# A fused two-layer graph network on one core: the passes through adj and layer 2 of groups 12 and 13 behind the last gates

## The chip, the cores and the metric

One Trainium2 chip, one of its cores. The time is the device time of one execution in microseconds (us), and it is given as the median of several runs. Engines are named as in the profile: PE is TensorE, DVE is VectorE, ACT is ScalarE, POOL is GpSimd, SP is SyncE, which only issues DMAs here.

## What is computed

64 graphs of 128 nodes with 128 features, all float32. `adj` is a symmetric 0/1 matrix for each graph.

```python
h = relu(layernorm(x))
# layer 1: a convolution over the nodes, messages between near nodes, and a gated unit
x_conv = relu(bn2(conv17(relu(bn1(conv1(h))))) + h)
s = h @ w_se.T + b_se;  A = exp(-squared_distances(s)) * adj
x_nmp = A @ relu(h @ w_msg.T + b_msg)
gi = [x_conv, x_nmp] @ w_ih.T + b_ih;  gh = h @ w_hh.T + b_hh
r, z = sigmoid(gi_r + gh_r), sigmoid(gi_z + gh_z)
x = x + (1 - z) * tanh(gi_n + r * gh_n) + z * h
# layer 2
h = relu(layernorm(x))
x = x + adj @ (h @ weight) + bias
```

## The kernel before

**Tiling.** The 64 graphs are 16 groups of four (NG = 16, GG = 4). A group is a tile of 128 x 512 (W = 512): the 128 partitions are nodes or features, and each 128 columns one graph. `x` and `adj` of a group come by one DMA of 256 KB each into rings of 8 and 6 slots; the result is built in the slot of `x` and stored from there. PSUM has eight banks of 128 x 512: pF, pH, pP, pQ, pZ, pI, and pN and pR, which are the two halves of the tensor pNR.

**Steps.** Each engine has a program of its own, in an order written out by hand, and the engines wait for each other by counting semaphores: `have(engine, s, n)` waits until s has reached n. After an opening come seven steps, t = 1 to 7. Step t does the convolution products and the gates of groups 2t and 2t + 1 ("middle"), the first part of groups 2t + 2 and 2t + 3 ("front"; there is none in step 7), and layer 2 of groups 2t - 2 and 2t - 1, called pp and qq. So step 7 does layer 2 of groups 12 and 13, and a function `ending` that of 14 and 15 (END = 15).

**Products** (`product`, L307; the matmuls are in `split_product`, L302 to 305). The convolution is nine products, each of 12 or 15 matmuls of 128 x 256 in three rounded parts. In step 7 PE's order is X22, X12, o_turn(13), X21, X23, adj_h2(12), X32, layer2(12), X11, adj_h2(13), X13, layer2(13), X31, X33, and then the gates of 14 and 15, each of 27 matmuls of 128 x 512. Two of these steps wait for more than their inputs. X11 waits for `between` on DVE (t_set), X31 for `scaled_third` on ACT (s32_set, L774), which reads bank pP before X31 overwrites it. ACT has second(13) ahead of it in its queue. Once the products are done, DVE adds the bases in two `conv_out` (L1101), of which the second needs POOL's last `sums` instruction (L1365).

**Layer 2 of a group** goes like this.
- `o_turn(g)` (PE, L468): four transposes of the gated result into pI or pH. It waits for `blend_end` (DVE, L1066 and L1068), which waits for `candidate` (ACT, L761), which waits for `blend_start` (DVE, L1056 to 1062).
- `residual(g)` (DVE, L1073) and `normalise2(g)` (DVE, L1079 to 1086) write x1 and its mean and variance, `scale2(g)` (POOL, L1302) the reciprocal root, `shift2(g)` (DVE, L1090) the bias `nb`, `second(g)` (ACT, L732, four instructions) the normalised h2[g % 2]. There are two buffers h2, so second(g) overwrites what layer2(g - 2) read.
- `adj_h2(g)` (PE, L475): the pass through adj, four matmuls into `back(g)`, which is pI for odd groups and pZ for even ones. `turned_up(g)` (ACT, L738) copies it back to h2[g % 2]. `layer2(g)` (PE, L483) multiplies by the weight, into the same bank.
- `with_bias(g)` (POOL, L1350) writes x1 plus the bias of layer 2 into the slot of `x`, `finish(g)` (DVE, L1096) adds the bank of layer2 to it, and SP stores the slot. SP's loop takes the groups in order.

In step 7 ACT's order is second(12), turned_up(12), second(13), scaled_third, turned_up(13), the gates. DVE's is ... shift2(12), normalise2(13), between, shift2(13), finish(12), finish(13), the gates.

**The ending.** The last group, 15, is done in two halves. On PE: 13 calls of `keep_clock` (L343, a matmul of 128 x 128 each, whose result nobody uses), o_turn(15), adj_h2(14), layer2(14), three calls of keep_clock, `end_pass` of both halves (L352, into pF and pQ), `end_layer2` of both halves (L361). On ACT: candidate(15), second(14), turned_up(14), the two halves of second(15) (L912), and the copies of their passes (L918, L920). On DVE: residual(14), normalise2(14), blend_start(15), shift2(14), blend_end(15), residual(15), normalise2_half(0) and (1) (L1241 to 1248), shift2_half(0) and (1) (L1252), finish(14), and the two last additions (L1270, L1272). On POOL: scale2(14), scale2_half(0), then, once DVE has written `nb` of half 0, scale2_half(1) (L1308), then, once `nb` of half 1 is there, with_bias(14) and with_bias(15).

In the profile a float32 matmul of 128 x 128 is recorded as two passes, so four of them are "x8"; a transpose is one.

Of the kernel before, what the change touches and what calls it, by code (L numbers as in the profile page):

```python
# [38 lines left out]
def gnn_kernel(nc, x_in, adj_in, vec_in, early_in, conv_in, gate_in, late_in, bias_in, out):  # L39
    ctx = ExitStack()  # L40
    with ctx:
# [147 lines left out]
        def graph(t, j):  # L189
            return t[:, j * N:(j + 1) * N]  # L190
# [3 lines left out]

        END = NG - 1

        end_pass_bank, end_out_bank = (pF, pQ), (pH, pP)

        def back(g):
            return (pI if g % 2 else pZ)[:]  # L200

        def two(t, e):
            return t[:, 2 * e * N:2 * (e + 1) * N]
# [97 lines left out]
        def _(pe):  # L301
# [43 lines left out]
            def end_pass(e):  # L345
                if e == 0:
                    pe.wait_ge(h2_half, 1)
                    have(pe, tz_set, END + 1)
                else:
                    have(pe, h2_set, END + 1)  # L350
                for j in (2 * e, 2 * e + 1):
                    last = pe.matmul(graph(end_pass_bank[e], j), graph(h2[END % 2], j), adjs(END, j), start=True, stop=True)  # L352
                last.then_inc(uT_done if e else uT_half_done, 1)

            def end_layer2(e):
# [62 lines left out]
            def gates_h(g):  # L418
                if g == 0:
                    pe.wait_ge(gate_split, 1)  # L420
                if g % 2 == 0:
                    have(pe, msg_set, min(g + 4, NG))
                    have(pe, out_set, g - 1)
                else:
                    have(pe, ghn_set, g)
                gate_part(pN, 2, 2, half(h_hi, g), half(h_lo, g), True, True).then_inc(hidden_done, 1)
                if g % 2:
                    have(pe, tr_set, g)
                gate_part(pR, 2, 0, half(h_hi, g), half(h_lo, g), True, False)
                if g == 0:  # L430
                    have(pe, nlo_set, 2)
                gate_part(z_bank(g)[:], 2, 1, half(h_hi, g), half(h_lo, g), True, False)
# [10 lines left out]
            def gates_n_i(g):  # L443
                if g % 2:
                    have(pe, v_set, g)
                else:
                    have(pe, out_set, g)
                gate_part(pI[:], 1, 2, half(n_hi, g), half(n_lo, g), True, False)

            def gates_c(g):  # L450
# [2 lines left out]
                gate_part(pR, 0, 0, m_hi, m_lo, False, True).then_inc(r_done, 1)  # L453
                gate_part(pI[:], 0, 2, m_hi, m_lo, False, True).then_inc(i_done, 1)
                gate_part(z_bank(g)[:], 0, 1, m_hi, m_lo, False, True).then_inc(z_done, 1)

            def back_bank(g):
                return pI if g % 2 else pZ

            def o_turn(g):  # L460
                have(pe, oT_set, g + 1)
# [9 lines left out]
            def adj_h2(g):  # L471
                have(pe, h2_set, g + 1)
                have(pe, tz_set, g + 1)
                for j in range(GG):
                    last = pe.matmul(graph(back_bank(g), j), graph(h2[g % 2], j), adjs(g, j), start=True, stop=True)  # L475
                last.then_inc(uT_done, 1)

            def layer2(g):
                if g == 0:
                    pe.wait_ge(late_loaded, 16)  # L480
                have(pe, uT_set, g + 1)
                for j in range(GG):
                    last = pe.matmul(graph(back_bank(g), j), graph(h2[g % 2], j), w_l1, start=True, stop=True)  # L483
                last.then_inc(l1_done, 1)

            def opening():
# [66 lines left out]
            def step(t):  # L553
                a, b, p, q, pp, qq = 2 * t + 2, 2 * t + 3, 2 * t, 2 * t + 1, 2 * t - 2, 2 * t - 1
                front, middle = t + 1 < NS, t < NS
                if t == 1:
                    pe.wait_ge(w_split, 6)
                if middle:
                    have(pe, cxlo_set, cx_before(t) + 1)
                    have(pe, ct_set, 2 * t)  # L560
                    product(pP, 0, X22, four(M22, True))
                if front:
                    x_turn(b)
                    conv1(a)
                    messages(a)
                if middle:
                    have(pe, cxlo_set, cx_before(t) + 2)
                    product(pP, 1, X12, four(M12, True)).then_inc(f_done[0], 1)
                o_turn(qq)
                if front:  # L570
                    conv1(b)
                    messages(b)
                    rows_turn(a)
                if middle:
                    have(pe, tz_set, 2 * t)
                    product(pQ, 0, X21, four(M21, True))
                if front:
                    distances(a)
                if middle:
                    have(pe, cxlo_set, cx_before(t) + 3)  # L580
                    product(pQ, 1, X23, four(M23)).then_inc(f_done[1], 1)
                adj_h2(pp)
                if front:
                    rows_turn(b)
                if middle:
                    have(pe, s1_set, t)
                    product(pP, 0, X32, four(M32)).then_inc(f_done[2], 1)
                layer2(pp)
                if middle:
                    have(pe, cxlo_set, cx_before(t) + 5)  # L590
                    have(pe, t_set, t)
                    product(pQ, 0, X11, four(A0, True))
                if front:
                    distances(b)
                    neighbour_sums(a)
                adj_h2(qq)
                if middle:
                    product(pQ, 1, X13, four(A2)).then_inc(f_done[3], 1)
                layer2(qq)
                if front:  # L600
                    neighbour_sums(b)
                if middle:
                    have(pe, s32_set, t)
                    product(pP, 0, X31, four(A1))
                    product(pP, 1, X33, four(A3)).then_inc(f_done[4], 1)
                    gates_h(p)
                    gates_n(p)
                    gates_c(p)
                    gates_h(q)
                    if t + 2 < NS:  # L610
                        x_turn(a + 2)
                    gates_n_rz(q)
                    if not front:
                        o_turn(p)
                    gates_n_i(q)
                    if front:
                        o_turn(p)
                    gates_c(q)

            def ending():  # L620
                have(pe, ct_set, 2 * NS)
                have(pe, xclo_set, 2 * NS)
                keep_clock(13)
                o_turn(END)
                adj_h2(END - 1)
                layer2(END - 1)
                keep_clock(3)
                end_pass(0)
                end_pass(1)
                end_layer2(0)  # L630
                end_layer2(1)
# [7 lines left out]
        def _(act):  # L639
# [227 lines left out]
            def step(t):  # L867
# [14 lines left out]
                if front:  # L882
                    decay(a)
                    messages(b)
                    left_rows(b)
                turned_up(pp)
                second(qq)
                if front:
                    split_hi(t + 1, 0)
# [3 lines left out]
                if front:  # L893
                    decay(b)
                    sums_hi(a)
                turned_up(qq)
                if t + 2 < NS:
                    first(a + 2)
                    first(b + 2)
# [3 lines left out]
                    gates(t)  # L903

            def ending():
                candidate(END)
                second(END - 1)
                turned_up(END - 1)
                for j in range(GG):
                    if j % 2 == 0:  # L910
                        act.wait_ge(nb2_set, END + 1 + j // 2)
                    last = act.activation(graph(h2[END % 2], j), graph(x1[END % 2], j), ACT.Relu,  # L912
                                          bias=nb2[END % 2][:, j:j + 1], scale=rs2[END % 2][:, j:j + 1])
                    if j == 1:
                        last.then_inc(h2_half, 1)
                last.then_inc(h2_set, 1)
                act.wait_ge(uT_half_done, 1)
                act.activation(two(h2[END % 2], 0), two(end_pass_bank[0], 0), ACT.Copy).then_inc(uT_half_set, 1)  # L918
                have(act, uT_done, END + 1)
                act.activation(two(h2[END % 2], 1), two(end_pass_bank[1], 1), ACT.Copy).then_inc(uT_set, 1)  # L920
# [28 lines left out]
        def _(dve):  # L949
# [119 lines left out]

            def residual(g):  # L1070
                have(dve, o_placed, g + 1)
                have(dve, out_set, g - 1)
                dve.scalar_tensor_tensor(x1[g % 2], (pI if g % 2 else pH)[:], 0.5, xs(g), ALU.mult, ALU.add)\  # L1073
                   .then_inc(x1_set, 1)

# [122 lines left out]
            def step(t):  # L1198
# [22 lines left out]
                shift2(qq)  # L1221
                if front:
                    right_rows(b)
                finish(pp)
                if front:
                    split_lo(t + 1, 0)
                    split_lo(t + 1, 1)
                    masked(b)
                    sums_lo(a)
                finish(qq)  # L1230
                if front:
                    sums_lo(b)
                if middle:
# [21 lines left out]
            def ending():  # L1255
# [6 lines left out]
                residual(END)  # L1262
                normalise2_half(0)
                normalise2_half(1)
                shift2_half(0)
                shift2_half(1)
                finish(p)
                have(dve, x1b_set, END + 1)
# [180 lines left out]
```

## Time and profile before

| | us |
|---|---|
| median of 3 runs | 347.70 |
| lowest and highest of them | 345.97 and 348.69 |
| the profiled execution | 345.98 |
| its span, first to last instruction | 344.1 |
| last gate's last matmul starts | 330.20 |
| last addition on DVE ends | 341.74 |

The times of the rows are counted from the start of the profiled execution's span. A row of a timeline gives the start, the length, the engine, the line of the kernel, the operation, the tiles written and read, how many such instructions are taken together, and in brackets how long the engine was idle before it and what ended the idle time. Buffer numbers are left out, so `work` stands for tr, tz, cand, zh, x1 and h2, and x_ring for any slot. The ends of matmuls are modelled and overlap the next start; starts are the better measure of PE's pace. The granted clock is the share of TensorE's full clock.

### The profile page before, as it was taken

The page shows a single profiled execution, that of the slowest core. Times are in us where ns is not written, and L with a number is a line of the kernel's source. Part 1 is how long each engine was busy: PE and PEld are TensorE (multiplying, and loading weights), DVE is VectorE, ACT ScalarE, POOL GpSimd, SP SyncE. Part 2 cuts the span into 40 slices and gives each one's busy share as a digit, 9 for nine tenths or more (in the row PEclk, how much of TensorE's full clock was granted, in tenths as well). Part 3 has the DMA queues.
Part 4 walks back from the last instruction along what each step waited for, and adds up shares of the span by engine and source line. Part 5 has one row for each costly group of instructions (what it writes and reads, how often), then busy time and mean ns, then how long its engine had stood idle before and what let it go on. Part 6 is the DMA issues. An engine that isn't in the chain of part 4 may idle for free.

```text
span 344.1 us, 6334 instructions
## 1 busy us (share of the span) xinstructions
PE 331.1 (96%) x2212; PEld 297.5 (86%) x2212; DVE 263.2 (76%) x735; ACT 220.8 (64%) x431; POOL 151.7 (44%) x131
## 2 busy tenths in 40 slices
PE   8699979999999999999999999999999999999995
PEld 5489968799989998899989998899989998899884
DVE  5597987898688976898688977898677968674473
ACT  2958745977775785667775785667776655452443
POOL 7053370035932297035922297036920396055014
PEclk9999999999999999999999999999999999999999
DMA  7900100001310031001210031001100000001001
GB/s 233 339 4 0 61 33 0 2 1 53 102 33 1 3 122 63 0 0 59 99 31 0 4 123 61 0 2 61 65 0 2 0 32 30 3 0 63 0 1 64
DMA packets 7952, 15.04 MB, mean 44 GB/s; under 512 B 1008, under 2 KB 1648, under 8 KB 7792
## 3 DMA queue, kind: packets, MB, share of 16 engines
q1 hardware_dynamic: 7776, 14.62, 12.4%
q8 instruction: 18, 0.29, 0.4%
q14 instruction: 14, 0.11, 0.1%
q10 hardware_dynamic: 144, 0.01, 0.0%
HBM read 10.43 MB, written 4.19 MB: 43 GB/s over the span
## 4 chain that ended last, share of the span: by engine, by line
issue 41%; POOL 30%; PE 13%; DVE 9%; ACT 5%; DMA 1%; POOLq 1%; DVEq 0%; ACTq 0%
POOL x_ring L1350 5%; POOL base L1362 3%; POOL rs L1297 3%; POOL ac L940 3%; POOL px L944 2%; POOL px L934 2%; POOL px L937 2%; POOL base L1365 2%; POOL rs L1302 2%; POOL base L1356 2%; DMA vec<-vec_in 1%; PE pNR L305 1%; PE pNR L303 1%; PE pNR L304 1%; ACT conv_hi L658 1%
## 5 line engine op out<-in xcount | busy, mean ns | idle before, releaser
L1302 POOL TENSOR_TENSOR rs<-ve,neg_half 128x4 f32<-128x4 f32 x15 | 15.6, 1039 | 94.7 <-DVE ve L1086 94.7
L1297 POOL TENSOR_TENSOR rs<-ve,neg_half 128x8 f32<-128x8 f32 (+1 forms) x9 | 15.5, 1720 | 73.0 <-DVE ve L964 73.0
L303 PE MATMUL pP<-cx_hi,conv_hi 128*128 128x256 f32 x154 | 45.1, 293 | 0.0
L305 PE MATMUL pP<-cx_hi,conv_lo 128*128 128x256 f32 x154 | 43.5, 282 | 0.0
L304 PE MATMUL pP<-cx_lo,conv_hi 128*128 128x256 f32 x154 | 43.3, 281 | 0.0
L303 PE MATMUL pQ<-cx_hi,conv_hi 128*128 128x256 f32 x126 | 37.2, 295 | 0.0
L305 PE MATMUL pQ<-cx_hi,conv_lo 128*128 128x256 f32 x126 | 35.4, 281 | 0.0
L304 PE MATMUL pQ<-cx_lo,conv_hi 128*128 128x256 f32 x126 | 35.4, 281 | 0.0
L732 ACT ACTIVATE work<-work,nb,rs 128x128 f32<-128x128 f32 x60 | 24.8, 483 | 15.1 <-DVE nb L1090 15.1
L303 PEld LDWEIGHTS pP<-cx_hi,conv_hi 128*128 128x128 f32 x154 | 29.1, 189 | 0.3
L304 PEld LDWEIGHTS pP<-cx_lo,conv_hi 128*128 128x128 f32 x154 | 29.1, 189 | 0.3
L305 PEld LDWEIGHTS pP<-cx_hi,conv_lo 128*128 128x128 f32 x154 | 29.0, 188 | 0.0
L1045 DVE TENSOR_TENSOR cx_lo<-px,cx_hi 128x576 fp32r<-128x576 f32 x28 | 27.2, 1009 | 0.8 <-ACT cx_hi L646 0.8
L304 PEld LDWEIGHTS pQ<-cx_lo,conv_hi 128*128 128x128 f32 x126 | 23.8, 189 | 0.3
L303 PEld LDWEIGHTS pQ<-cx_hi,conv_hi 128*128 128x128 f32 x126 | 23.8, 189 | 0.0
L305 PEld LDWEIGHTS pQ<-cx_hi,conv_lo 128*128 128x128 f32 x126 | 23.7, 188 | 0.0
L752 ACT ACTIVATE work<-pNR,rz_b 128x512 f32<-128x512 f32 x16 | 11.0, 689 | 19.5 <-PE pNR L305 19.0
L665 ACT ACTIVATE hn<-x_ring,nb,rs 128x128 f32<-128x128 f32 x56 | 22.5, 485 | 0.0
L1350 POOL TENSOR_TENSOR x_ring<-work,late 128x512 f32<-128x512 f32 x16 | 20.4, 1278 | 0.3 <-DVE nb L1252 0.3
L1096 DVE TENSOR_TENSOR x_ring<-pI,x_ring 128x512 f32<-128x512 f32 x7 | 4.8, 692 | 20.2 <-POOL x_ring L1350 15.9
L646 ACT ACTIVATE cx_hi<-px 128x576 fp32r<-128x576 f32 x28 | 17.6, 674 | 3.6 <-POOL px L942 3.1
L761 ACT ACTIVATE work<-work,vec 128x512 f32<-128x512 f32 x16 | 11.6, 724 | 11.4 <-DVE work L1059 11.4
(275 smaller groups left out, 1071.7 us busy)
## 6 DMA issues: line engine op xcount, KB each, us to landing
x_ring<-x_in SPq DMA_DIRECT2D x16, 256.0 KB, 2.8
adj_ring<-adj_in SPq DMA_DIRECT2D x16, 256.0 KB, 3.0
out<-x_ring SPq DMA_DIRECT2D x15, 256.0 KB, 2.0
work<-conv_in SPq DMA_DIRECT2D x1, 1088.0 KB, 8.0
x_ring<-gate_in SPq DMA_DIRECT2D x1, 576.0 KB, 7.6
out<-x_ring SPq DMA_DIRECT2D x2, 128.0 KB, 1.8
early<-early_in SPq DMA_DIRECT2D x1, 129.5 KB, 3.4
late<-late_in SPq DMA_DIRECT2D x1, 128.0 KB, 7.9
```

What stands on the lines that cost most here:

```text
L303: pe.matmul(acc, w_hi, m_hi, start=start, stop=False)
L304: pe.matmul(acc, w_hi, m_lo, start=False, stop=False)
L305: return pe.matmul(acc, w_lo, m_hi, start=False, stop=stop)
L646: act.activation(cx_hi[:, CX_PARTS[k][0]:CX_PARTS[k][1]], cx_source(k), ACT.Copy).then_inc(cxhi_set, 1)
L665: last = act.activation(graph(hn[g % 2], j), xs(g, j), ACT.Identity, bias=nb1[:, i:i + 1], scale=rs1[:, i:i + 1])
L732: last = act.activation(graph(h2[g % 2], j), graph(x1[g % 2], j), ACT.Relu, bias=nb2[g % 2][:, j:j + 1], scale=rs2[g % 2][:, j:j + 1])
L752: act.activation(tr, pR, ACT.Tanh, bias=rz_b[:, 0:1], scale=0.5).then_inc(tr_set, 1)
L761: act.activation(cand[g % 2], cand[g % 2], ACT.Tanh, bias=vec[:, V_IN:V_IN + 1], scale=1.0)\
L1045: dve.tensor_tensor(cx_lo[:, part], cx_source(k), cx_hi[:, part].bitcast(F32), ALU.subtract)\
L1297: pool.tensor_tensor(rs1[:, lane], ve1[:, lane], neg_half[:, lane], ALU.pow).then_inc(rs1_set, 1)
L1302: pool.tensor_tensor(rs2[g % 2][:], ve2[g % 2][:], neg_half[:, 0:GG], ALU.pow).then_inc(rs2_set, 1)
L1350: pool.tensor_tensor(xs(g).rearrange("p (g d) -> p g d", g=GG), x1[g % 2].rearrange("p (g d) -> p g d", g=GG), l1_bias, ALU.add).then_inc( ...
```

## The change

Layer 2 of groups 12 and 13 (LATE) is begun but not finished in step 7. Both passes through adj go behind the last gates on PE, both layer2 behind them, in place of most of the filler; ACT's copies and DVE's finishes go to the ending too. The passes get banks of their own, pN for group 12 and pF for group 13, so the last pass of group 15 takes pR instead of pF. Waits for out_set in the gates and in residual are changed accordingly.

The first `ending` below is PE's, the second ACT's, the third DVE's; in `step` the same condition stands before turned_up on ACT and finish on DVE, for pp and for qq.

```diff
-        end_pass_bank, end_out_bank = (pF, pQ), (pH, pP)
+        end_pass_bank, end_out_bank = (pR, pQ), (pH, pP)
+        LATE = (END - 3, END - 2)
+        def back_bank(g):
+            if g in LATE:
+                return (pN, pF)[g % 2]
+            return pI if g % 2 else pZ
         def back(g):
-            return (pI if g % 2 else pZ)[:]
+            return back_bank(g)[:]
...
             def gates_h(g):
-                    have(pe, out_set, g - 1)
+                    have(pe, out_set, g - 1 if g < END - 1 else g - 3)
             def gates_n_i(g):
-                    have(pe, out_set, g)
+                    have(pe, out_set, g if g < END - 1 else g - 2)
             def adj_h2(g):
                 have(pe, h2_set, g + 1)
                 have(pe, tz_set, g + 1)
+                if g in LATE:
+                    have(pe, nlo_set, NG)
+                    have(pe, ghn_set, NG)
...
             def step(t):
-                adj_h2(pp)
+                if pp not in LATE:
+                    adj_h2(pp)
-                layer2(pp)
+                if pp not in LATE:
+                    layer2(pp)
...
             def ending():
+                adj_h2(END - 3)
+                adj_h2(END - 2)
                 have(pe, ct_set, 2 * NS)
                 have(pe, xclo_set, 2 * NS)
-                keep_clock(13)
+                keep_clock(2)
+                layer2(END - 3)
+                keep_clock(4)
                 o_turn(END)
+                layer2(END - 2)
                 adj_h2(END - 1)
                 layer2(END - 1)
                 keep_clock(3)
...
             def ending():
+                turned_up(END - 3)
                 candidate(END)
+                turned_up(END - 2)
+                have(act, l1_done, END - 2)
                 second(END - 1)
                 turned_up(END - 1)
+                have(act, l1_done, END - 1)
...
             def residual(g):
-                have(dve, out_set, g - 1)
+                have(dve, h2_set, g - 1)
+                have(dve, x1b_set, g - 1)
...
             def ending():
                 normalise2_half(0)
                 normalise2_half(1)
+                finish(END - 3)
                 shift2_half(0)
+                finish(END - 2)
                 shift2_half(1)
                 finish(p)
```

## Rows read from the trace of the kernel before

**Rows 1.** The page, its first part: busy time and share of each engine.
```profile
PE 331.1 (96%) x2212; PEld 297.5 (86%) x2212; DVE 263.2 (76%) x735; ACT 220.8 (64%) x431; POOL 151.7 (44%) x131
```

**Rows 2.** Windows of the ending: length, then each engine's busy time, granted clock, DMA.
```profile
330.40:333.70 3.30, 3.10 (x27) 2.87 (x25) 3.06 (x6) 2.91 (x6) 1.20 (x1) 1.00 0.00 0
333.70:341.30 7.60, 6.05 (x42) 5.10 (x42) 3.66 (x15) 3.10 (x8) 3.88 (x4) 1.00 0.01 3
```

**Rows 3.** Timeline of PE, last step: start, length, what, idle time before it.
```profile
305.58 0.28 PE L304 MATMUL pQ<-cx_lo,conv_hi 128*128 128x256 f32 x1
305.70 0.28 PE L305 MATMUL pQ<-cx_hi,conv_lo 128*128 128x256 f32 x1
306.20 1.16 PE L475 MATMUL pZ<-adj_ring,work 128*128 128x128 f32 x8 [0.22 <-ACT work L732]
307.12 0.36 PE L303 MATMUL pP<-cx_hi,conv_hi 128*128 128x256 f32 x1
...
308.63 1.05 PE L483 MATMUL pZ<-late,work 128*128 128x128 f32 x8
309.44 0.36 PE L303 MATMUL pQ<-cx_hi,conv_hi 128*128 128x256 f32 x1
309.64 0.28 PE L304 MATMUL pQ<-cx_lo,conv_hi 128*128 128x256 f32 x1
```

**Rows 4.** Timeline of PE, ending.
```profile
330.43 3.06 PE L343 MATMUL pP<-ident 128*128 128x128 f32 x26
333.70 0.75 PE L468 MATMUL pI<-ident,work 128*128 128x128 f32 x4 [0.21 <-DVE work L1068]
334.29 1.06 PE L475 MATMUL pZ<-adj_ring,work 128*128 128x128 f32 x8
336.03 1.16 PE L483 MATMUL pZ<-late,work 128*128 128x128 f32 x8 [0.69 <-ACT work L738]
337.03 0.83 PE L343 MATMUL pP<-ident 128*128 128x128 f32 x6
338.12 0.71 PE L352 MATMUL pF<-adj_ring,work 128*128 128x128 f32 x4 [0.26 <-ACT work L912]
```

**Rows 5.** Timeline of ACT, last step and ending.
```profile
309.82 0.55 ACT L774 ACTIVATE s<-pP,bn_half,bn_a 128x256 f32<-128x256 f32 x1
...
331.48 0.72 ACT L761 ACTIVATE work<-work,vec 128x512 f32<-128x512 f32 x1 [0.16 <-DVE work L1059]
332.15 1.65 ACT L732 ACTIVATE work<-work,nb,rs 128x128 f32<-128x128 f32 x4
335.38 0.60 ACT L738 ACTIVATE work<-pZ 128x512 f32<-128x512 f32 x1 [1.58 <-PE pZ L475]
337.19 0.88 ACT L912 ACTIVATE work<-work,nb,rs 128x128 f32<-128x128 f32 x2 [1.21 <-DVE nb L1252]
```

**Rows 6.** Timeline of POOL, last step and ending.
```profile
312.12 1.29 POOL L1365 TENSOR_TENSOR base<-base,s 128x512 f32<-128x512 f32 x1
...
337.49 0.70 POOL L1308 TENSOR_TENSOR rs<-ve,neg_half 128x2 f32<-128x2 f32 x1 [0.53 <-DVE nb L1252]
338.46 2.49 POOL L1350 TENSOR_TENSOR x_ring<-work,late 128x512 f32<-128x512 f32 x2 [0.27 <-DVE nb L1252]
```

**Rows 7.** Timeline of DVE, last step and ending.
```profile
314.74 0.69 DVE L1096 TENSOR_TENSOR x_ring<-pI,x_ring 128x512 f32<-128x512 f32 x1 [4.32 <-PE pI L483]
315.35 0.75 DVE L1101 SCALAR_TENSOR_TENSOR pQ<-pQ,bn_a,base 128x512 f32<-128x512 f32 x1
...
317.57 0.76 DVE L1101 SCALAR_TENSOR_TENSOR pP<-pP,bn_a,base 128x512 f32<-128x512 f32 x1
...
332.96 0.69 DVE L1068 TENSOR_TENSOR work<-work 128x512 f32<-128x512 f32 x1
...
336.99 0.16 DVE L1252 SCALAR_TENSOR_TENSOR nb<-mv,rs 128x2 f32<-128x2 f32 x1
```

**Rows 8.** The page, its last part: DMA issues, size, time to landing.
```profile
out<-x_ring SPq DMA_DIRECT2D x15, 256.0 KB, 2.0
```

More of the change, by code:

```diff
@@ L348, in end_pass @@
                     have(pe, tz_set, END + 1)
+                    have(pe, tr_set, END + 1)
                 else:
@@ L351, in end_pass @@
                 for j in (2 * e, 2 * e + 1):
-                    last = pe.matmul(graph(end_pass_bank[e], j), graph(h2[END % 2], j), adjs(END, j), start=True, stop=True)
+                    last = pe.matmul(graph(end_pass_bank[e][:], j), graph(h2[END % 2], j), adjs(END, j), start=True, stop=True)
                 last.then_inc(uT_done if e else uT_half_done, 1)
@@ L455, in gates_c @@
                 gate_part(z_bank(g)[:], 0, 1, m_hi, m_lo, False, True).then_inc(z_done, 1)
-            def back_bank(g):
-                return pI if g % 2 else pZ
             def o_turn(g):
@@ L473, in adj_h2 @@
                 have(pe, tz_set, g + 1)
+                if g in LATE:
+                    have(pe, nlo_set, NG)
+                    have(pe, ghn_set, NG)
                 for j in range(GG):
-                    last = pe.matmul(graph(back_bank(g), j), graph(h2[g % 2], j), adjs(g, j), start=True, stop=True)
+                    last = pe.matmul(graph(back(g), j), graph(h2[g % 2], j), adjs(g, j), start=True, stop=True)
                 last.then_inc(uT_done, 1)
@@ L482, in layer2 @@
                 for j in range(GG):
-                    last = pe.matmul(graph(back_bank(g), j), graph(h2[g % 2], j), w_l1, start=True, stop=True)
+                    last = pe.matmul(graph(back(g), j), graph(h2[g % 2], j), w_l1, start=True, stop=True)
                 last.then_inc(l1_done, 1)
@@ L595, in step @@
                     neighbour_sums(a)
-                adj_h2(qq)
+                if qq not in LATE:
+                    adj_h2(qq)
                 if middle:
                     product(pQ, 1, X13, four(A2)).then_inc(f_done[3], 1)
-                layer2(qq)
+                if qq not in LATE:
+                    layer2(qq)
                 if front:
@@ L885, in step @@
                     left_rows(b)
-                turned_up(pp)
+                if pp not in LATE:
+                    turned_up(pp)
                 second(qq)
@@ L895, in step @@
                     sums_hi(a)
-                turned_up(qq)
+                if qq not in LATE:
+                    turned_up(qq)
                 if t + 2 < NS:
@@ L1223, in step @@
                     right_rows(b)
-                finish(pp)
+                if pp not in LATE:
+                    finish(pp)
                 if front:
@@ L1229, in step @@
                     sums_lo(a)
-                finish(qq)
+                if qq not in LATE:
+                    finish(qq)
                 if front:
```

## The prediction

> **What bounds the kernel now.** I read the page first. PE is busy for 331.1 of 344.1 us, 96%, and no other engine is above 76% [rows 1], so matmul time that leaves PE's queue should come off the span wherever no other engine is just behind it. The timeline of PE in the last step (t = 7) bears this out: pieces of products follow each other every 0.12 us, and the only idle time around the first moved pass is 0.22 us before 306.20 [rows 3]. The ending is another regime. In its first 3.3 us PE counts as busy for 3.10, but 26 of its 27 passes there are filler; in the following 7.6 us it is busy for 6.05 and waits for DVE once and for ACT again and again [rows 2, 4]. So the ending is a chain that runs through several engines, and PE's work there is free only up to its filler and its waits. In the two timelines of POOL and DVE the reader should see the chain's last links: the second reciprocal root at 337.49, which waited for DVE's `nb` of 336.99, and then the two bias additions, 2.49 us from 338.46 [rows 6, 7].
>
> All times below are on the clock of before; the shift that the last step gives is taken off at the end.
>
> **Part 1: 16 matmuls leave the last step.** adj_h2(12), layer2(12), adj_h2(13) and layer2(13) are four matmuls each, recorded as eight passes. What one costs is read from the starts around it. L305 at 305.70 would be followed by the next product 0.12 later, at 305.82. Instead there is the pass from 306.20 and X32 begins at 307.12, and the first matmul behind such a block takes 0.20 instead of 0.12 (309.44 to 309.64), so 0.08 more: 307.12 + 0.08 - 305.82 = 1.38 us, the wait for h2 included. The second goes from 308.63 to 309.44, plus 0.08: 0.89 us [rows 3]. The third and the fourth look the same. Sum: 1.38 + 3 x 0.89 = **4.05 us**.
>
> Can the last step use it? Three things could be late next.
> - Product X31 begins 1.38 + 0.89 + 0.89 = 3.16 us earlier, at 310.45, and must have s32, which ACT writes from 309.82 for 0.55, so until 310.37 [rows 5]. With the 0.05 us from engine to engine (DVE ends at 332.96 + 0.69, PE starts at 333.70 [rows 4, 7]) that is 310.42: 0.03 us to spare. ACT does not come to it sooner, because it first has the normalisation of group 13.
> - DVE's second conv_out stands at 317.57 behind the last product; 4.05 earlier is 313.52. POOL's sum for it starts at 312.12 and takes 1.29, until 313.41 [rows 6, 7]. 0.1 us to spare.
> - The finishes of 12 and 13 leave DVE ahead of conv_out (314.74, the next at 315.35, so 0.61 us each [rows 7]); DVE waited 4.32 us there, so this brings nothing more.
> So I take the full 4.05, with almost no reserve. The gates behind it move together with what they wait for. Their waits on out_set are lowered by as much as the finishes are moved, and cost nothing. The two waits that residual has in place of its one on out_set are fulfilled whenever DVE comes to them; I take 0, and at most 0.1 for the additional wait in the ending.
>
> **Part 2: the same passes in PE's ending.** The filler's pass rate: 26 passes last 3.06, 6 last 0.83, so one takes (3.06 - 0.83) / 20 = 0.111 us [rows 4]. Before, 13 fillers are 26 passes from 330.43, 2.9 us, issued by 333.3; then o_turn(15) waits for DVE until 333.70. Now there are 8 + 8 (both passes through adj), 4 (two fillers), 8 (layer2(12)) and 8 (four fillers) ahead of o_turn: 36 passes, 4.0 us, issued by 334.43. Is anything else later than that? The first pass through adj is done at 330.43 + 7 x 0.111 + 0.27 (the tail of a pass, 0.83 - 5 x 0.111) = 331.48. ACT then copies uT(12), 331.52 to 332.12 at the 0.60 of its row at 335.38, and only behind it candidate(15), which stood at 331.48 [rows 5]. An ACT instruction starts a little before the one ahead of it ends (331.48 + 0.72 = 332.20, the next at 332.15), so I put it at 332.04: 0.56 us late. DVE's end of the blend, 332.96 for 0.69 [rows 7], is late by the same and releases o_turn at 333.70 + 0.56 = 334.26. That is before 334.43, so PE's own queue decides: o_turn starts **0.73 us later**. Bounds: 0.56 (DVE alone) and 1.05 (if four changes of kind cost 0.08 each, as behind the blocks of rows 3). I take 0.73 because all of these passes are of the filler's kind. layer2(12) does not stall PE: uT(12) is there at 332.12, and PE comes to it at 332.65.
>
> **Part 3: ACT and PE between o_turn and the halves of group 15.** second(14) now waits for layer2(12), done at 333.54 + 0.16 = 333.70; it starts at 333.74, 1.59 later than at 332.15, and ends at 335.39 [rows 5]. PE meanwhile does o_turn (0.59, 333.70 to 334.29 [rows 4]) and layer2(13), 0.89, until 335.91, and the pass of group 14 until 336.80. ACT copies it, 337.01 to 337.61; layer2(14) takes PE 1.00 (336.03 to 337.03 [rows 4]) from 337.64, and three fillers 0.67, until 339.31. The first half pass of group 15, which must not be late, stood at 338.12; by the sum of parts 2 and 4 it is due at 339.46. That leaves 0.15 us of the cover. I take 0; if turned-up copies and passes each cost a little more, 0.1 to 0.4 us.
>
> **Part 4: finish(12) stands ahead of `nb` on DVE.** At 336.99 DVE came straight from the variance and wrote `nb` of the first half [rows 7]. Now finish(12), 0.61 us to the next start (314.74 to 315.35), goes first: **0.61 us**. Behind `nb` wait ACT's first half (337.19), and POOL's second root (337.49), then POOL's bias additions and the last finishes, so nothing hides it. finish(13) lies in the time in which POOL computes the second root, 0.70 us, and is hidden: DVE has it done at about 339.1 and the root at 339.5. Bounds of this term: 0.69, and 0.35, since POOL started 0.34 after `nb` ended [rows 6, 7], where other engines need 0.05; if some 0.26 of that is POOL's own preparation, it absorbs that much. The POOL part is one chain of two, so I take 0.61.
>
> **Part 5: stores.** The outputs of 12 and 13 now leave at about 338.4 and 339.1, with some 2.0 us each to landing [rows 8], and those of 14 and 15 from 341.9. They are gone, or nearly, when the last half is issued at 343.1. I take 0, at most 0.3.
>
> **The sum.** The profiled execution took 345.98 us, with 1.9 us around its span of 344.1. 345.98 - 4.05 + 0.73 + 0.61 = **343.3 us**, a ratio of 0.992. The median of the three runs shown is 347.7, 0.5% above the profiled one; 347.7 x 0.992 = **345.0 us**.
>
> **The rivals.**
> *The last step does not give its 4.05 us.* s32 (0.03 to spare) or POOL's sums hold the products up. For it: these margins. Against: a late sum of POOL is caught before gates_c, which does not need it until more than 1 us later. A loss goes one for one; with 0.7 us lost, 344.0 profiled and 345.7 us.
> *The ending hides everything.* If o_turn and `nb` had room that the timelines don't show, all 4.05 us would arrive: 341.9 profiled, 343.6 us. For it: a third of the ending is waits and filler [rows 2]. Against: parts 2 and 4 each found a queue with nothing between.
> *Slower: PE's clock falls in the ending.* Real passes stand where an unbroken row of 26 filler passes stood, and now PE waits for ACT between them. The granted clock is 1.00, the 2.4 GHz level, in both windows of the ending, although PE is idle there for 1.5 of 7.6 us [rows 2]. Were it at the 1.2 GHz level from the gates on, the 36 passes would take 4.0 us more. Then o_turn, layer2(13), the pass, layer2(14) and three fillers, 34 passes or 3.8 us more, and 8 passes of the halves, 0.9 us: 345.98 - 2.7 + 8.7 = 352.0 profiled, 353.7 us. It decides from 2.7 / 0.111 = 24 slow passes on. Against: the new waits, 0.8 us at most, are hardly longer than the 0.69 of before [rows 4].
> The Trainium skill (TensorE: Matmul & The Clock Gate, section "What's actually happening") speaks for this rival: "the default state is throttled, and activity releases the throttle". The waits of 0.2 to 0.7 us in rows 4 did not bring the clock down, so this trace does not show the fall.
>
> **How the numbers follow.** The forecast gets 0.73, the last step's loss 0.12, the full gain 0.10, the clock 0.05. The bounds of the terms give gains from 1.6 us (1.05 and 0.69 lost, 0.4 in part 3, 0.3 elsewhere) to 3.1 us (0.56 and 0.35 lost). On the median that is 344.6 to 346.1, and the three runs of before lie 1.7 below and 1.0 above their median; together with the full gain, the range is 342.5 to 347.6 us. One per cent, 3.5 us, is about what a measurement of this kernel can tell from no change. The forecast's 2.7 us is under it, and by scatter passes it one time in four (0.19); with most of the full gain (0.08) and a little of the second case that is 0.28 for faster. Slower by over 1% is the clock alone, 0.04. Within 1%: 0.68.
>
> **What would show it.** In the last step PE's starts around X32, X11, X13 and X31 without the blocks, the first filler-like pass at 326.4, and no new wait ahead of X31. In the ending, o_turn(15) 4.0 us behind the end of the gates rather than 3.3 (3.8 would say that DVE decides). ACT's candidate(15) straight behind the copy of pN. DVE: finish(12) between the variance and `nb`, 0.61 us. A wait of PE ahead of the first half pass of under 0.2 us. Wrong would be: an idle PE in front of X31, a granted clock below 1.00 behind the gates, or a first half pass that follows the fillers without a wait, which would mean that part 3 has become the bound.

## The result, and the profile after

The median of 16 runs is 345.52 us, against 347.72 us for 16 runs of the kernel before beside them: 2.20 us less. The runs of a kernel lie in steps some 1.5 us apart, and the two middle runs of the changed kernel, 345.04 and 346.01, lie on either side of such a step, so this difference is a poor measure. The ratio of the two kernels is 0.9918, with an interval from 0.9899 to 0.9936, and that is 2.85 us; it leaves out one run of the changed kernel, which at 348.26 us was a slow one. The forecast was 345.0 us and a ratio of 0.992.

The profiled execution took 344.95 us with a span of 342.6, so only 1.5 us less than that of before. To compare the two, one has to know first where the clock of each was low. ACT's `scaled_first` of the last step, ahead of everything that the change touches, in the timeline of ACT of the kernel before and then of the changed one:

```profile
302.32 0.56 ACT L767 ACTIVATE s<-pP,bn_half,bn_a 128x256 f32<-128x256 f32 x1 [2.01 <-PE pP L305]
```

```profile
303.84 0.56 ACT L785 ACTIVATE s<-pP,bn_half,bn_a 128x256 f32<-128x256 f32 x1 [2.00 <-PE pP L313]
```

The changed kernel comes there 1.52 us later. The windows of its opening say why (length, busy time and count of PE, PEld, DVE, ACT, POOL, granted clock, DMA share, GB/s):

```profile
14.00:18.00 4.00, 1.87 (x12) 1.53 (x11) 3.83 (x6) 3.94 (x7) 0.00 (x0) 1.00 0.61 228
18.00:22.00 4.00, 4.00 (x13) 3.09 (x12) 3.75 (x28) 0.76 (x2) 1.38 (x1) 0.57 0.02 4
22.00:26.00 4.00, 4.00 (x24) 3.47 (x23) 2.21 (x6) 1.99 (x4) 3.92 (x4) 1.00 0.01 2
```

From 18 to 22 us the granted clock was 0.57 on average: mostly its 1.2 GHz level, behind a stretch in which PE was busy for 1.87 of 4 us. In the profile of before it is 1.00 in the same windows, with the same wait of 2.13 us ahead of them. Other runs of before show such steps too, so I don't put this down to the edit of the last step; the experiments come back to it. The 1.52 us are taken out of the comparison, and 344.1 + 1.52 - 342.6 = 3.02 us is what the change gained between the two profiles.

The ending of the changed kernel in PE's timeline (start, length, what; it answers to [rows 4]):

```profile
327.98 1.05 PE L484 MATMUL pNR<-adj_ring,work 128*128 128x128 f32 x8
328.86 1.06 PE L484 MATMUL pF<-adj_ring,work 128*128 128x128 f32 x8
329.76 0.61 PE L351 MATMUL pP<-ident 128*128 128x128 f32 x4
330.20 1.06 PE L492 MATMUL pNR<-late,work 128*128 128x128 f32 x8
331.10 1.06 PE L351 MATMUL pP<-ident 128*128 128x128 f32 x8
331.99 0.64 PE L474 MATMUL pI<-ident,work 128*128 128x128 f32 x4
...
335.11 1.16 PE L492 MATMUL pZ<-late,work 128*128 128x128 f32 x8 [0.69 <-ACT work L756]
336.10 0.83 PE L351 MATMUL pP<-ident 128*128 128x128 f32 x6
336.93 0.52 PEld L361 LDWEIGHTS pNR<-adj_ring,work 128*128 128x128 f32 x4 [0.19 <-ACT work L936]
336.93 0.71 PE L361 MATMUL pNR<-adj_ring,work 128*128 128x128 f32 x4
```

From `scaled_first` to the end of the gates it is 28.11 us before (302.32 to 330.43) and 24.14 us now (303.84 to 327.98), so the last step gave 28.11 - 24.14 = 3.97 us. o_turn(15) stands 4.01 us behind the gates, without a wait, instead of 3.27: **0.74 us lost** to PE's own queue. The first half pass of group 15 shows no wait in PE's row, where it had 0.26 us, but that is the modelled end of the fillers: at 0.111 us for each of the six passes from 336.10 PE would have come to it at 336.77, and it started at 336.93, together with its weight load, which waited for ACT. So 0.16 us of the cover are left.

ACT's timeline ([rows 5]):

```profile
329.06 0.60 ACT L756 ACTIVATE work<-pNR 128x512 f32<-128x512 f32 x1 [0.20 <-PE pNR L484]
329.56 0.71 ACT L779 ACTIVATE work<-work,vec 128x512 f32<-128x512 f32 x1
...
331.30 1.65 ACT L750 ACTIVATE work<-work,nb,rs 128x128 f32<-128x128 f32 x4 [0.54 <-PE pNR L492]
```

The candidate stands straight behind the copy, 1.58 us behind the gates instead of 1.05, and second(14) waits for layer2(12), 3.32 behind the gates instead of 1.72.

DVE's timeline, and then POOL's, between the variance and the last addition ([rows 6, 7]):

```profile
335.15 0.69 DVE L1121 TENSOR_TENSOR x_ring<-pNR,x_ring 128x512 f32<-128x512 f32 x1
335.76 0.15 DVE L1279 SCALAR_TENSOR_TENSOR nb<-mv,rs 128x2 f32<-128x2 f32 x1
335.82 0.68 DVE L1121 TENSOR_TENSOR x_ring<-pF,x_ring 128x512 f32<-128x512 f32 x1
336.72 0.16 DVE L1279 SCALAR_TENSOR_TENSOR nb<-mv,rs 128x2 f32<-128x2 f32 x1 [0.21 <-POOL rs L1337]
...
339.83 0.41 DVE L1301 TENSOR_TENSOR x_ring<-pP,x_ring 128x256 f32<-128x256 f32 x1
```

```profile
335.99 0.70 POOL L1337 TENSOR_TENSOR rs<-ve,neg_half 128x2 f32<-128x2 f32 x1 [0.84 <-DVE nb L1279]
```

finish(12) lies ahead of `nb` as forecast. From o_turn to `nb` it is 3.77 us instead of 3.29, **0.48 lost**: 0.61 by the two starts above, less 0.11 by which o_turn is shorter when PE comes to it without a wait (0.64 against 0.75), and less 0.02 that I can't place. POOL's root follows `nb` after 0.23 instead of 0.50, start to start: **0.27 absorbed**. From the root to the last addition it is 3.84 us in both, and from that addition's end to the end of the span 2.36 in both, so the stores cost nothing. The account: -3.97 + 0.74 + 0.48 - 0.27 = -3.02.

### The profile page after: what moved, and what is told of

It reads as the page before. It is cut to its first block, busy times and chain, and to the rows that moved or that the text cites. A ratio compares the mean times of both kernels' runs of the same rounds, so it can differ in the third digit from the quotient of the medians.

```text
span 342.6 us, 6310 instructions
## 1 busy us (share of the span) xinstructions
PE 329.8 (96%) x2198; PEld 296.3 (86%) x2198; DVE 261.6 (76%) x735; ACT 220.5 (64%) x431; POOL 152.1 (44%) x131
## 4 chain that ended last, share of the span: by engine, by line
PE 65%; DVE 19%; ACT 9%; issue 4%; POOL 1%; DMA 1%; POOLq 0%; DVEq 0%; ACTq 0%
PE pQ L311 4%; PE pQ L312 4%; PE pQ L313 4%; PE pNR L311 4%; PE pNR L313 4%; PE pNR L312 4%; PE pF L424 4%; PE pP L311 4%; PE pP L312 4%; PE pP L313 4%; DVE st L981 3%; ACT work L750 2%; PE pZ L484 2%; PE pI L313 2%; PE pI L311 2%
## 5 line engine op out<-in xcount | busy, mean ns | idle before, releaser
L399 PEld LDWEIGHTS pNR<-early,hn 128*128 128x128 f32 x128 | 16.3, 189 | 3.0 <-issue 2.1
```

Source lines behind the costliest of these rows:

```text
L399: last = pe.matmul(ms[:, j, 0:MS], graph(hn[g % 2], j), w_ms, start=False, stop=True, skip_group_check=True)
```

## The experiments

Positions in a trace are counted from the ending's first pass through adj (327.98 in the profile above), so that the clock of the opening does not enter. In the changed kernel o_turn(15) is at 4.01 and the last addition at 11.85.

### The ending: e1, e2, e4

e1_finish_behind:

```diff
-                finish(END - 3)
                 shift2_half(0)
-                finish(END - 2)
                 shift2_half(1)
+                finish(END - 3)
+                finish(END - 2)
```

> The changed kernel with finish(12) and finish(13) behind both shift2 halves on DVE. My theory: finish(12) ahead of the first `nb` holds it up by 0.59 us, of which POOL's own preparation absorbs 0.27, so the last addition comes 0.3 us earlier, counted from the first pass through adj of the ending; the two finishes fit in the 1.45 us in which DVE waits for POOL's bias additions. Rival 1: POOL follows `nb` whenever it comes, then the whole 0.6 us is gained. Rival 2: the stores of 12 and 13 now run together with those of 14 and 15 and give it back behind the last addition, 0.3 us or more. Time: 0.1% less than the changed kernel, which cannot be told in the time, only in the trace.

DVE and then POOL in its timelines; its first pass is at 328.14:

```profile
335.34 0.16 DVE L1279 SCALAR_TENSOR_TENSOR nb<-mv,rs 128x2 f32<-128x2 f32 x1
...
339.68 0.42 DVE L1301 TENSOR_TENSOR x_ring<-pP,x_ring 128x256 f32<-128x256 f32 x1
```

```profile
335.82 0.70 POOL L1337 TENSOR_TENSOR rs<-ve,neg_half 128x2 f32<-128x2 f32 x1 [0.52 <-DVE nb L1279]
```

`nb` comes 7.20 behind the first pass instead of 7.78, 0.58 earlier, but the root then starts 0.32 behind its end instead of 0.08. The last addition is at 11.54: 0.31 us earlier, not 0.6. So rival 1, the whole 0.6 us, falls. From the last addition's start to the span's end it is 2.82 us (342.5 - 339.68) instead of 2.77: rival 2 has 0.05 us. (Ratio to before 0.9884, interval 0.9855 to 0.9913.)

e2_no_filler:

```diff
                 layer2(END - 3)
-                keep_clock(4)
                 o_turn(END)
```

> The changed kernel without the four fillers ahead of o_turn(15). My theory: PE's queue decides o_turn, by little; without the 8 passes (0.9 us) DVE decides, and o_turn comes 0.2 us earlier (DVE was done at 331.72, o_turn stood at 331.99), not 0.9. Rival 1: the filler was the whole delay, then 0.7 to 0.9 us are gained. Rival 2: PE's clock falls behind a gap of 0.7 us, then the granted clock in the ending is below 1.00 and the time 1 to 5 us longer.

PE's timeline, with the first pass at 326.53, and the windows behind the gates:

```profile
330.33 0.75 PE L474 MATMUL pI<-ident,work 128*128 128x128 f32 x4 [0.52 <-DVE work L1091]
```

```profile
326.40:330.30 3.90, 3.41 (x30) 3.18 (x28) 3.16 (x6) 2.83 (x6) 1.29 (x1) 1.00 0.00 2
330.30:338.20 7.90, 6.94 (x50) 5.99 (x50) 4.79 (x17) 4.21 (x11) 3.89 (x4) 1.00 0.18 67
```

o_turn waits for DVE again and comes at 3.80, 0.21 us earlier. By the last addition (338.28, so 11.75) 0.10 of it is left, because the o_turn behind a wait takes 0.75 again. The clock stays at 1.00 up to PE's last matmul. Both rivals fall; the ratio, 0.9926 (0.9902 to 0.995), cannot tell 0.1 us.

e4_full_filler has `keep_clock(11)` in that place.

> The changed kernel with 11 fillers instead of 4 ahead of o_turn(15), so 13 calls in all, as before the change. My theory: o_turn stands in PE's own queue, so 14 passes cost 1.55 us one for one: ratio to the kernel before 0.9962 instead of 0.9918, and the wait of PE ahead of the first half pass is no longer. Rival (the ending hides what PE does there): under 0.5 us.

PE's timeline; the first pass is at 328.32:

```profile
333.90 0.64 PE L474 MATMUL pI<-ident,work 128*128 128x128 f32 x4
```

o_turn at 5.58, 1.57 us later, and the last addition (341.75) at 13.43, 1.58 later. One for one: the ending hides none of it. The ratio was 0.9933 (0.9908 to 0.9959), and the expected 0.9962 lies just outside: by the times alone the cost would be less than by the trace. Of its six runs two had a clock of 1.00, spans 342.8 and 343.0, against 341.1 for the one such run of the changed kernel, and that agrees with the trace.

### The last step alone: e3, e8

e3_last_step_alone, an edit of the kernel before:

```diff
-                for j in range(GG):
+                for j in range(GG if g not in (END - 3, END - 2) else 1):
                     last = pe.matmul(graph(back_bank(g), j), graph(h2[g % 2], j), adjs(g, j), start=True, stop=True)
```

and the same in layer2.

> The kernel before, with one matmul in place of four in each of adj_h2(12), layer2(12), adj_h2(13) and layer2(13), everything else in its place: 12 of the 16 matmuls are left out (three of four graphs of groups 12 and 13 are not computed), and the ending is untouched. My theory: the last step gives one for one: 24 passes of 0.111 us, 2.7 us, ratio 0.992. Rival: the last step is held by ACT's s32 or POOL's sums, then there is an idle PE ahead of X31 and the gain is 2 us or less.

From adj_h2(12) to the first filler it is 24.23 us in the kernel before (306.20 to 330.43). Here, in PE's timeline:

```profile
308.12 0.49 PE L475 MATMUL pZ<-adj_ring,work 128*128 128x128 f32 x2 [0.22 <-ACT work L732]
...
321.49 0.50 PE L303 MATMUL pNR<-xc_hi,gate_hi 128*128 128x512 f32 x1 [0.42 <-DVE xc_lo L1105]
...
330.45 3.06 PE L343 MATMUL pP<-ident 128*128 128x128 f32 x26
```

22.33 us, a gain of 1.90, not 2.66; ratio 0.9952 (0.9931 to 0.9973). PE waits in front of gates_c(14) for DVE, but not for the reasons that the prediction feared. DVE's timeline:

```profile
316.69 0.69 DVE L1096 TENSOR_TENSOR x_ring<-pI,x_ring 128x512 f32<-128x512 f32 x1 [5.72 <-POOL x_ring L1350]
317.30 0.75 DVE L1101 SCALAR_TENSOR_TENSOR pQ<-pQ,bn_a,base 128x512 f32<-128x512 f32 x1
```

finish(13) stands in DVE's queue ahead of conv_out and waits for POOL's with_bias(13), which is behind all of POOL's sums. So the products were ready and their additions were not made. The trace of before already had this, in POOL's timeline:

```profile
313.36 1.27 POOL L1350 TENSOR_TENSOR x_ring<-work,late 128x512 f32<-128x512 f32 x1
```

It ends at 314.63, and PE's layer2(13), which the row of finish(13) names as what it waited for, at 313.61 + 1.05 = 314.66. POOL was only 0.03 us ahead of PE, so with PE's part taken away the wait would hardly have been shorter. e8_finish13_later leaves e3 as it is and moves that one instruction:

```diff
             def step(t):
-                finish(qq)
+                if middle and not front:
+                    pass
+                else:
+                    finish(qq)
...
             def gates(t):
                 conv_lo_out(t, 1)
+                if t == NS - 1:
+                    finish(2 * t - 1)
```

> The kernel of e3_last_step_alone (12 of the 16 matmuls in the last step left out, three of four graphs of groups 12 and 13 not computed) with finish(13) on DVE behind both conv_out and conv_lo_out of step 7 instead of ahead of them. e3 gained about 1.9 us where 2.7 were expected; its trace shows PE idle for 0.42 us in front of gates_c(14), and DVE's finish(13) waiting for POOL's with_bias(13) until 316.6. My theory: finish(13), not the products, held the conv_out behind it, so that the change of the study gained its 4 us only because it took the finishes out of the way too; here the wait in front of gates_c goes and the executions at full clock have a span of 341.5 (2.7 less than 344.2), or 343.1 with one stretch of low clock. Rival: POOL's sums or ACT's s32 hold the step, then the span stays at about 342.2 and 343.9.

PE's timeline:

```profile
309.49 0.49 PE L475 MATMUL pZ<-adj_ring,work 128*128 128x128 f32 x2 [0.23 <-ACT work L732]
...
322.31 0.40 PE L303 MATMUL pNR<-xc_hi,gate_hi 128*128 128x512 f32 x1
...
331.17 3.06 PE L343 MATMUL pP<-ident 128*128 128x128 f32 x26
```

The wait is gone and the stretch is 21.68 us: 2.55 less than before, against the 2.66 of 24 passes. The ratio was 0.9892 (0.9853 to 0.9931). None of its four runs had a clock of 1.00 throughout, so the span of 341.5 wasn't seen; the nearest, at 0.998, has 341.9, and the two at 0.994 have 343.0 and 343.3 for the 343.1 that was expected. So the last step does give one for one, or nearly, but only where finish(13) is no longer ahead of conv_out in DVE's queue. (finish(12) stayed where it was.)

How near the next limit was shows in the changed kernel itself, ACT's s32 and PE around the start of X31:

```profile
311.34 0.55 ACT L792 ACTIVATE s<-pP,bn_half,bn_a 128x256 f32<-128x256 f32 x1
```

```profile
311.86 0.28 PE L313 MATMUL pQ<-cx_hi,conv_lo 128*128 128x256 f32 x1
311.98 0.35 PE L311 MATMUL pP<-cx_hi,conv_hi 128*128 128x256 f32 x1
312.16 0.28 PE L312 MATMUL pP<-cx_lo,conv_hi 128*128 128x256 f32 x1
```

s32 is written at 311.89, and X31 starts 0.12 us behind the matmul ahead of it, as without a wait; its own first matmul takes 0.06 us longer than the others. No run moves s32 by itself.

### The clock of the opening: e5, e6, e7, e9, f1, f2

The runs of each kernel lie about 1.5 us apart, and the mean granted clock goes with it. Of the 16 runs of the changed kernel one has 1.00 and a span of 341.1, seven 0.995 and 342.5 to 342.9, seven 0.99 and 344.1 to 344.4, one 0.988 and 346.5. Where the clock falls, by the windows of e1's profile (0.99, the two stretches):

```profile
10.00:14.00 4.00, 3.25 (x11) 2.48 (x12) 0.69 (x1) 4.00 (x8) 0.00 (x0) 0.73 1.03 402
14.00:18.00 4.00, 3.49 (x21) 3.17 (x21) 3.77 (x5) 3.94 (x8) 0.00 (x0) 0.84 0.55 205
48.00:52.00 4.00, 3.02 (x14) 2.97 (x15) 2.44 (x16) 2.61 (x5) 3.04 (x3) 0.67 0.00 0
52.00:56.00 4.00, 4.00 (x19) 3.28 (x18) 2.21 (x5) 1.11 (x2) 0.00 (x0) 0.90 0.00 0
```

PE has two waits of some 2 us there: for the first products, until 17, and for distances(3), until 49. The second stretch, from 49.3, lies right behind the second wait. So does, in the profile of the changed kernel, the stretch from 18.3 behind the first wait (2.13 us, until 16.87). But the first stretch of e1 lies ahead of that wait, from 11.9 to 15.3, behind waits of 0.2 to 0.75 us; PE's row of the first products:

```profile
17.02 0.47 PE L337 MATMUL pQ<-cx_hi,conv_hi 128*128 128x512 f32 x1 [0.51 <-DVE cx_lo L1063]
```

They start when they do in the kernel before, at 17.04 there, so that stretch cost nothing: the slow fillers used up the wait. e5_opening_after and e6_opening_before fill the first wait:

```diff
                 messages(0)
-                keep_clock(6)
+                keep_clock(15)
                 pe.wait_ge(w_split, 1)
```

> The changed kernel with 15 fillers instead of 6 in the opening, ahead of the first products: 18 more passes, 2.0 us, in the 2.1 us in which PE waits there. In the profiled run of the changed kernel the granted clock was 0.58 and 0.57 from 18 to 22 us and 1.00 around it, the step of 1.52 us by which the last step begins later than in the profiled run of before. My theory: the wait and the thin work around it let the clock fall for a stretch in most runs, and with the filler it does not: runs at 341 us of span, the fastest of before the edit, and a median some 1.5 to 3 us less. Rival 1: the clock falls by something that the filler does not touch, then the runs keep their spans at 341, 342.6 and 344.2. Rival 2: the filler delays the first products and costs 0.2 to 1 us.

> The same edit of the opening alone, in the kernel before. My theory: its runs lie 1.5 us apart for the same reason (345.97, 347.6 and 349.1), so the median falls by the same amount, to about 346, ratio 0.995 or less; the changed kernel with the same edit stays 2.7 to 3.0 us below it. Rival: no difference, the scatter of before has another cause.

e5: 343.17 us, ratio 0.9866 (0.9824 to 0.9909), three of four runs at 1.00 with spans of 341.2 to 341.4. e6: 345.98 us, ratio 0.9951 (0.9923 to 0.9979), seven of eight at 1.00 with 344.1 to 344.3. The filler costs nothing: 344.1 is the span of before at 1.00. So both medians fell because fewer runs had a stretch of low clock. Between the two, 345.98 - 343.17, it is 2.81 us, where 2.7 to 3.0 were expected. In e6 the second wait was still there, 2.04 us in its profile, and yet only one of eight runs had a stretch, so the wait alone does not bring the clock down.

e7_all_three has the edits of e5, e1 and e2 together.

> The changed kernel with the filler of the opening, without the four fillers ahead of o_turn(15), and with the finishes behind the halves. My theory: 0.2 + 0.3 us from the ending and 1.5 to 3 us from the opening, so 2 to 3.5 us less than the changed kernel, ratio to before 0.983 to 0.986. Rival: the gap in the ending lets the clock fall there and takes back 1 us or more.

343.39 us, ratio 0.9859 (0.9827 to 0.9891). Its last addition (338.00, first pass at 326.57) is at 11.43, 0.42 us earlier than in the changed kernel, and three runs at 1.00 have 340.8. The rival, a clock that falls in the ending, did not come. The other three are at 0.995 and 342.3 or 342.4, so a stretch of low clock still came in half of them. e9_second_gap adds

```diff
-                distances(3)
-                neighbour_sums(2)
                 direct(15)
+                distances(3)
+                neighbour_sums(2)
```

> The kernel of e7_all_three with direct(15) ahead of distances(3) and neighbour_sums(2) in the opening. In the profiles with a second stretch of low clock it lies at 48 to 54 us, behind PE's wait of 2.0 to 2.2 us for distances(3) at 49. direct(15), nine matmuls and 1.5 us, is ready and can lie in that wait. My theory: the wait shrinks to some 0.6 us, the work behind it comes 1.4 us earlier and the low clock at 48 to 54 us does not come again: nearly all executions at a clock of 1.00 and a span of 339.4, median 341.2. Rival 1: POOL or ACT hold the first step anyway and the 1.4 us are lost again, span 340.8. Rival 2: the low clock comes elsewhere, then spans 1.5 us apart remain.

PE's timeline in place of the wait of 2.03 us:

```profile
47.80 0.40 PE L339 MATMUL pP<-cx_hi,conv_lo 128*128 128x512 f32 x1
48.85 0.50 PE L415 MATMUL pH<-right,left 128*128 128x512 f32 x1 [0.65 <-ACT left L736]
```

All six runs have 0.999 or 1.00, spans of 339.5 to 339.8, and the median is **341.50 us**, ratio 0.9804 (0.9778 to 0.9829): the fastest version here. With the clock steady, the change of this study can be measured to a tenth: f1_steady_before and f2_steady_after are the two kernels with both edits of the opening and nothing else.

> The kernel before with both edits of the opening (15 fillers ahead of the first products, direct(15) ahead of distances(3)) and nothing else. My theory: these edits take away the stretches of low clock, whatever stands in the ending: all executions within 0.3 us of each other, span 342.8 (344.2 less 1.4), time 344.7. Rival: the executions keep lying 1.5 us apart, as in the kernel before.

> The changed kernel with the same two edits. My theory: span 339.8, time 341.7, so that the change of the study is worth 3.0 us (0.87%) when the clock is out of the comparison, and the two small edits of the ending (e1, e2) are worth 0.4 us less than nothing of noise: e9 is 0.3 to 0.4 us below this one. Rival: 2.7 us, as forecast without POOL's absorption; or the change had been faster only by the chance of its runs' clocks, then under 2 us.

f1: 344.78 us, eleven of twelve runs between 344.64 and 345.04 (one at 0.993 and 346.21). f2: 341.83 us, six runs between 341.68 and 342.01. The change is worth 344.78 - 341.83 = **2.95 us**, 0.86%, and e1 and e2 together the 0.33 us by which e9 is below f2, although these two were not run side by side. Both profiles of the pair are at full clock, 0.999 and 1.00, so the account of the result can be made again with nothing taken out: from `scaled_first` to the end of the gates 28.09 and 24.13 us, from there to o_turn 3.27 and 4.01, to `nb` 3.29 and 3.77, to POOL's root 0.51 and 0.23, to the last addition 3.84 in both. That is -3.96 + 0.74 + 0.48 - 0.28 = -3.02 us once more.

Of the 18 runs of e5, e6 and e7, with the filler alone, 13 were at 1.00; of the kernel before, in the four sets of runs beside the experiments, 10 of 60. Of the 24 runs of e9, f1 and f2, with both edits of the opening, all but one were at 0.998 or more. The filler's effect is beyond chance. That direct(15) adds to it is likely, but 5 runs of 18 against 1 of 24 don't prove it, and no run has direct(15) alone. It also takes 1.2 us off the span at full clock (e7 to e9, 340.8 to 339.6), where 1.4 were expected.

## Why the prediction was right

**Part 1, the last step:** 4.05 forecast, 3.97 measured. X31 did have its 0.03 us to spare, nearly (0.06 lost). One sentence of this part was wrong: that the departure of the finishes from DVE's queue "brings nothing more". e3 and e8 show that for finish(13) it is a condition of the gain. Between adj_h2(12) and the filler it was worth 0.65 us already with 12 of the 16 matmuls away. I had read DVE's wait of 4.32 us at finish(13) as time to spare. But conv_out stands behind that instruction, and with the products 4 us earlier finish(13) would have waited until 314.63 for POOL. That the full gain came is in this respect luck: the change had to move finish(13) only because its input comes later.

**Part 2, PE's filler:** 0.73 forecast, 0.74 measured; e4 shows one for one, and e2 that DVE stands 0.21 us behind, for a forecast difference of 0.17.

**Part 3:** second(14) is the 1.6 us late that were forecast, and it costs nothing. The candidate is 0.53 late, for 0.56. The cover of the first half pass was put at 0.15 us, and by the starts it is 0.16. PE's row without a wait looks like the sign of being wrong that the prediction named, but it isn't: ACT released that pass. In e1, where `nb` is earlier, PE and not ACT's half decides that pass (8.79 behind the first pass, no wait), but the end is set by POOL.

**Part 4, finish(12):** 0.61 forecast and 0.61 measured for the instruction, of which POOL absorbed 0.27. I had named this as the lower bound and not taken it. With o_turn's 0.11, and less the 0.08 of part 1, it makes the difference between the 2.7 us of the sum and the 3.0 of the two profiles. So the forecast of the gain was 10% low, and of the terms this is the one that was mis-sized. e1 shows it from the other side: 0.58 us taken away gave 0.31.

**Part 5, the stores:** 0, as forecast.

**The range and the median.** The bounds and the scatter that the prediction names give 342.9 to 347.1 us; it wrote 342.5 to 347.6 without saying where the rest comes from. The forecast median of 345.0 is the ratio put on the median of three runs. That the median of all 16 came out within 0.5 us of it owes something to chance, since it depends on how many runs had a stretch of low clock; the gain of 2.95 us between f1 and f2 does not.

**The rivals.** Of "the ending hides everything" 0.27 us was true. The last step's loss would have been real with finish(13) left in place. The fall of the clock in the ending did not come: it was 1.00 from the gates to PE's last matmul, in e2 also behind a wait of 0.52 us. The sentence that stood beside it (the Trainium skill, TensorE: Matmul & The Clock Gate, "What's actually happening") fits the opening of these kernels better, and there the traces agree in part: behind PE's waits of 2.13 us (changed kernel) and 2.02 us (e1) the granted clock fell, but in the profile of before it stayed at 1.00 behind waits of 2.13 and 2.03 us. The one profiled execution on which the prediction rests was one of the few at full clock throughout. The scatter from 345.97 to 348.69, which the range took as chance, is mostly these stretches; two edits of the opening remove nearly all of it and bring the kernel before from 347.56 to 344.78 us (f1), about as much as the change of this study.

## What to carry to other kernels

Work taken from the bound engine counts one for one only if the waits that stood behind it in other engines' queues go with it: look for an instruction that waits for something late in a queue in front of one that is needed early. A row names only what ended a wait last, so look also at what was due just before it. Work put in place of filler is not free once it is longer than the filler; compare its passes with the slack of the wait behind it. Where an engine starts later behind its releaser than others do, as POOL here (0.34 us, others 0.05), a part of a delay can be absorbed (0.27 of 0.61 us). Where runs of a kernel lie in steps, look at the granted clock of each run before measuring small changes, and fill or reorder the waits ahead of the place where it falls.

## What I had not expected

One stretch of low clock costs 1.5 to 1.7 us and two cost 3.1 to 3.2, by spans of 344.1, 345.8 and 347.3 in the kernel before at mean clocks of 1.00, 0.995 and 0.99. But a stretch costs only what PE can't spare: in e1's profile the first one lay where PE has filler and a wait, and its two stretches together cost 1.6 (342.5 against 340.9). What decides in which runs the clock falls is not shown. Behind waits of up to 0.7 us in the ending it did not fall in any profile. POOL's second root started 0.32 to 0.34 us behind `nb` when `nb` came early, and 0.08 behind it when it came 0.6 us later; I take that to be its sequencer at work on the waits that precede the instruction, which no run here tells apart from another cause. And DVE's `nb` of group 13, at 306.98 in the kernel before, took 1.24 us where the median of its 15 instructions is 0.16; a bias addition of POOL ran beside it, from 306.92 for 1.29. second(13) and s32 wait behind it, so the reserve of 0.03 us ahead of X31 may be larger if the two are pulled apart; no run tries that.
